# One kernel, one change: attention weights divided by each head's largest coefficient, the product with V in four column groups, and multiply-adds and tanh over two key blocks at a time

## What is computed

```python
q = (x @ Wq.T + bq).reshape(B, L, H, hd).transpose(0, 2, 1, 3)   # k, v likewise
sim = jnp.einsum('bhid,bhjd->bhij', q, k) / jnp.sqrt(hd) / (abs(temperature)[0] + 0.1)
scores = 0
for fi, freq in enumerate([31.0, 37.0, 41.0, 43.0, 47.0]):
    scores = scores + alpha[h, fi] * jnp.sin(TWO_PI * sim / freq + phi[h, fi])
w = jax.nn.sigmoid(scores)
w = w / (jnp.sum(w, axis=-1, keepdims=True) + 1e-10)
out = jnp.einsum('bhij,bhjd->bhid', w, v)                         # then Wo, bo, layer norm
```

## Time and profile before

| | us |
|---|---|
| median of 3 runs (7797.35 to 7801.88) | 7801.56 |
| the profiled execution | 7801.02 |
| its span in the trace | 7799.3 |
| projection and setup, to the first fill | 467.9 |
| attention, 467.9 to 6921.0 | 6453.1 |
| last stage | 878.3 |

### The profile page before, as it was taken

How to read it: one execution, slowest core, us unless ns; L and a number is a source line. 1 busy time by engine, 2 the same in 40 slices (tenths; PEclk the granted TensorE clock), 3 DMA queues, 4 the chain that set the end, 5 groups by cost and what they waited for, 6 DMA issues and landing times. The chain is left out here.

```text
span 7799.3 us, 138640 instructions
## 1 busy us (share of the span) xinstructions
PE 6920.1 (89%) x48057; PEld 4266.5 (55%) x48057; DVE 6862.6 (88%) x7370; ACT 5959.1 (76%) x6386; POOL 155.7 (2%) x217
## 2 busy tenths in 40 slices
PE   6459999999999999999999999999999999955555
PEld 3235555555555555555555555555555555534554
DVE  5659999999999999999999999999999999967775
ACT  1058888888888888888888888888888888841112
POOL 0000000000000000000000000000000000000000
PEclk8779999999999999999999999999999999976666
DMA  7921111111111111111111111111111111121110
GB/s 305 355 73 39 38 39 40 40 39 38 38 38 38 40 40 40 39 38 38 37 38 40 40 40 38 38 38 37 38 40 40 39 38 37 38 52 39 40 40 18
DMA packets 312136, 420.90 MB, mean 54 GB/s; under 512 B 156084, under 2 KB 185684, under 8 KB 311064
## 3 DMA queue, kind: packets, MB, share of 16 engines
q1 hardware_dynamic: 306712, 414.98, 16.8%
q0 software_dynamic: 5376, 5.30, 0.3%
HBM read 275.19 MB, written 144.83 MB: 54 GB/s over the span
## 5 line engine op out<-in xcount | busy, mean ns | idle before, releaser
L562 DVE SCALAR_TENSOR_TENSOR a_weight<-a_wave,a_head_c,a_weight 128x1024 f32<-128x1024 f32 x4096 | 5263.3, 1285 | 426.7 <-ACT a_wave L537 286.6
L537 ACT ACTIVATE a_wave<-a_ps_turn 128x1024 f32<-128x1024 f32 x5120 | 4926.0, 1033 | 733.2 <-PE a_ps_turn L465 733.2
L465 PE MATMUL a_ps_turn<-a_q_r,a_k_r 64*128 64x512 f32 x20480 | 3768.0, 413 | 308.6 <-ACT a_wave L537 204.9
L465 PE MATMUL a_ps_turn<-a_q_r,a_rounder 64*128 64x512 f32 x20480 | 3206.4, 391 | 0.0
L465 PEld LDWEIGHTS a_ps_turn<-a_q_r,a_k_r 64*128 64x128 f32 x20480 | 1922.3, 184 | 2170.2 <-ACT a_wave L537 1567.0
L465 PEld LDWEIGHTS a_ps_turn<-a_q_r,a_rounder 64*128 64x128 f32 x20480 | 1931.9, 185 | 271.2
L531 ACT ACTIVATE a_weight<-a_weight 128x1024 f32<-128x1024 f32 x1024 | 1097.0, 1071 | 2.4 <-DVE a_weight L562 2.4
L485 PE MATMUL a_ps_out<-a_weight,a_v_r 128*32 128x512 f32 x4096 | 1077.3, 605 | 3.9 <-ACT a_weight L531 2.4
L586 DVE TENSOR_SCALAR a_weight<-a_wave,a_head_c 128x1024 f32<-128x1024 f32 x1024 | 764.5, 747 | 55.9 <-ACT a_wave L537 55.9
L485 PEld LDWEIGHTS a_ps_out<-a_weight,a_v_r 128*32 128x32 f32 x4096 | 147.5, 107 | 376.1 <-ACT a_weight L531 328.8
L444 POOL COPY a_head_c<-a_table 128x5 f32 (+1 forms) x128 | 64.3, 503 | 6332.7 <-DVE a_weight L562 6332.7
(11 more groups left out here) (210 smaller groups left out, 1895.7 us busy)
## 6 DMA issues: line engine op xcount, KB each, us to landing
q_d<-p_q_hl SPq DMA_DIRECT2D x80, 1024.0 KB, 8.5
a_q_r<-q_d SPq DMA_DIRECT2D x256, 320.0 KB
a_k_r<-k_d SPq DMA_DIRECT2D x512, 128.0 KB
a_q_r<-q_d SPq DMA_DIRECT2D x256, 160.0 KB
k_d<-p_k_hl SPq DMA_DIRECT2D x8, 4096.0 KB, 15.5
a_k_r<-k_d SPq DMA_DIRECT2D x512, 64.0 KB
o_d<-a_out SPq DMA_DIRECT2D x256, 34.0 KB
p_x_in<-in_L_attn_x SPq DMA_DIRECT2D x8, 1024.0 KB, 17.4
```

What stands on the lines that cost most here:

```text
L465: last = nc.tensor.matmul(ps_turn[SLOT[f]][:, half, :], exact(w(rows[half])), exact(q_r[rows[half], k, f, :]), start=(i == 0), stop=(i == 3))
L537: nc.scalar.activation(wave[:, s % 2, f, :], ps_turn[SLOT[f]][:].rearrange("p a b -> p (a b)"), ACT.Sin, scale=TURN_IN).then_inc(sines, 1)
L562: return v.scalar_tensor_tensor(weight[:, s % RING, :], wave[:, s % 2, f, :], head_c[:, k, f:f + 1], weight[:, s % RING, :], ALU.mult, ALU ...
```

## The change

1. **Coefficients.** A chain of 45 small steps on DVE at the start of `project_qkv` makes a table `tab` of 16 heads: the frequency with the largest |alpha| changes places with frequency 0, and alpha, 1/freq and phi with it; the other four coefficients are divided by that largest one, and in place 0 stands half of it. The phases' reduction, until now seven steps in the attention's setup, is part of the chain. The scale of q comes from a tile `rate` with one column a frequency, which SP loads back through HBM, instead of constants.
2. **Multiply-adds.** The wave in place 0 has the coefficient 1, so its scaling goes: the first multiply-add takes wave 1 times its coefficient plus wave 0. `wave` and `weight` hold two units (a pair), and each of the four multiply-adds of a pair runs over 2048 columns. The wait is for the sine of the pair's second unit.
3. **tanh** runs over 2048 columns in place, with the scale read from `head_c` (half of the largest coefficient). It stands between sines 3 and 4 of the odd units.
4. **The product with V** is issued in the even units, for the pair two back: four matmuls, two units times two halves of the queries, each to its own 32 columns of the array. `ps_out` and `out` use 128 partitions; `o_d` holds two sums a head, which the last stage loads separately and adds: den in one small addition and num in one of 2048 columns.

The order of fills and sines is unchanged.

```diff
+                for i in range(3):
+                    step(v.tensor_tensor(work[0], tab[:, i, :], first, ALU.mult))
+                    step(v.tensor_tensor(work[1], tab[:, i, :], other, ALU.mult))
+                    step(v.tensor_copy(work[2][:, 0:1], tab[:, i, 0:1]))
+                    step(v.tensor_reduce(tab[:, i, 0:1], work[0], AX.X, ALU.add))
+                    step(v.scalar_tensor_tensor(tab[:, i, 1:NF], first[:, 1:NF], work[2][:, 0:1], work[1][:, 1:NF], ALU.mult, ALU.add))
...
-                        nc.vector.tensor_scalar(q_hl[:, f, 0, :].bitcast(F32R), whole, 1.0 / FREQS[f], None,
+                        nc.vector.tensor_scalar(q_hl[:, f, 0, :].bitcast(F32R), whole, rate[:, m, f:f + 1], None,
                                                 ALU.mult).then_inc(q_step, 1)
...
-                    for j in range(2):
-                        last = nc.tensor.matmul(ps_out[VP * j:VP * (j + 1), :], v_r[:, k, t, :],
-                                                weight[:, t % RING, halved(j)], start=(t == 0), stop=(t == U - 1))
+                    for c in range(4):
+                        last = nc.tensor.matmul(ps_out[VP * c:VP * (c + 1), :], v_r[:, k, t + c // 2, :],
+                                                weight[:, t // 2, c // 2, halved(c % 2)], start=(t == 0), stop=(t == U - 2))
                     last.then_inc(weighted, 1)
...
-                        if s >= 2 and main(g):
-                            times_v(n - 2, s - 2, g, k)
-                        if s < 2 and after(g):
-                            times_v(n - 2, U - 2 + s, g - 1, 1 - k)
+                        if s in (4, 6) and main(g):
+                            times_v(PAIRS * g + s // 2 - 2, s - 4, g, k)
+                        if s in (0, 2) and after(g):
+                            times_v(PAIRS * g + s // 2 - 2, U - 4 + s, g - 1, 1 - k)
...
-                            if f == 4 and (after(g) or s >= 1) and (main(g) or s == 0):
-                                act.wait_ge(summed, n)
-                                tile = weight[:, (s - 1) % RING, :]
-                                nc.scalar.activation(tile, tile, ACT.Tanh, scale=0.5).then_inc(squashed, 1)
+                            if f == 4 and s % 2 and (after(g) or s > 1) and (main(g) or s == 1):
+                                p = PAIRS * g + s // 2 - 1
+                                act.wait_ge(summed, p + 1)
+                                tile = weight[:, (s // 2 - 1) % PAIRS, :, :].rearrange("p a l -> p (a l)")
+                                nc.scalar.activation(tile, tile, ACT.Tanh, scale=head_c[:, k if s > 1 else 1 - k, 0:1]).then_inc(squashed, 1)
...
+                    for i in range(PAIRS):
+                        n, p = g * U + 2 * i + 1, g * PAIRS + i
+                        if i == 2 and after(g):
+                            dve.wait_ge(weighted, PAIRS * g)
                             wait_pos(dve, stored[1 - k], stores_before(g, k))
-                            v.tensor_copy(out[:, 1 - k, :], ps_out[0:2 * VP, :]).then_inc(out_ready, 1)
+                            v.tensor_copy(out[:, 1 - k, :], ps_out[:]).then_inc(out_ready, 1)
...
+                            wait_pos(dve, weighted, p - RING + 1)
+                            dve.wait_ge(sines, NF * n + 2)
+                            add_wave(i, k, 1, both(wave[:, i % 2, 0, :, :])).then_inc(added, 1)
+                            for f in range(2, NF):
                                 dve.wait_ge(sines, NF * n + f + 1)
-                                add_wave(n, s, k, f).then_inc(added, 1)
+                                dve.wait_ge(added, 3 * p + f - 1)
+                                add_wave(i, k, f, both(weight[:, i, :, :])).then_inc(summed if f == NF - 1 else added, 1)
...
+                        step_f(v.tensor_tensor(den[:, 2, :], den[:, 0, :], den[:, 1, :], ALU.add))
+                        step_f(v.tensor_scalar(den[:, 3, :], den[:, 2, :], float(L), 2 * EPS_DEN, ALU.add, ALU.add))
+                        v.reciprocal(den[:, 4, :], den[:, 3, :]).then_inc(S["den_ready"], 1)
+                        step_f(v.tensor_tensor(flat(num[:, 0, :, :]), flat(num[:, 0, :, :]), flat(num[:, 1, :, :]), ALU.add))
```

168 lines of the change are left out of this document (94 added, 74 removed).

## The result

The median of four runs of the changed kernel is 8204.31 us (8202.87 to 8205.89), against 7799.87 us for the kernel before (four runs, 7797.35 to 7801.88): a ratio of 1.0519, 95% interval 1.0501 to 1.0537. The forecast was 8195.

What follows compares the result with a forecast made beforehand. Bound taken: PE's loop through PSUM slot 1, 6.30 us a key block, not PE's total work. Attention +371, projection +4 and +7, last stage +10, together 392 more than 7801: 8193, rounded 8195 us; range 8085 to 8380 us.

Steps and rivals of the forecast that it cites:

- The PE loop and the ACT loop through slot 1: Attention, per key block: PE's fills, product and sine 1, 6.30 us; ACT's sines, tanh and fill 1, 6.01 us, hidden.
- The odd unit: Attention, a pair's key block with the wide tanh and no product: 6.94 us, PE idle 1.6 us before fill 1.
- The even unit: Attention, a pair's key block with the product and no tanh: stays at 6.30 us, product in four groups 0.98 us.
- The copy's wait: Attention, PE's first product of a head waits for DVE's copy of the last head's result: 0.36 us a head.
- DVE's 2.5 us a pair worth nothing: Attention: wider multiply-adds and dropped scalings save DVE about 2.5 us a pair, which gains nothing, as DVE wasn't the bound.
- The attention: Whole attention stage: 53.3 us a head, 2.9 more, over 128 heads +371 us.
- The projection: Projection stage: +4 us for the coefficient steps before PE's first turn of x, +7 us for pointer operands.
- The last stage: Stage after attention: extra loads and additions of den and num, +10 us, between 5 and 30.
- Rival (b): Attention: PE's work is the bound, not the loop, so a pair takes 11.62 us; 7320 us in all, chance 0.07.
- Rival (a): Product with V: four column groups don't run at once, product 1.84 us, +440 us, 8635 in all; chance 0.09.
- rival (c): Attention: no change, the pair stays at 12.60 us, tanh 0.64 us shorter than forecast; 7822 us in all, chance 0.02.
- Rival (d): Attention: PE's granted clock falls to 1.2 GHz as PE idles, +9.3 us a pair, some 12900 us; chance 0.01.

Runs made afterwards that it cites:

- e1: Changed kernel with the product with V moved from the even units to the odd ones, which have the tanh: 7555.7 us, ratio 0.9687 to the kernel before.
- e3: Changed kernel with the tanh moved from before sine 4 of the odd unit to behind it: 8017.9 us, ratio 1.0281 to the kernel before.
- e9: Changed kernel with fills in the order of the sines, PSUM slots 0, 1, 2 in turn, product behind an odd unit's fill: 7100.3 us.
- e6: Changed kernel with eight multiply-adds of 1024 columns a pair instead of four of 2048: 8199.9 us, ratio 1.0518 to the kernel before.
- e11: Changed kernel with PSUM slots in turn (e9), with eight multiply-adds of 1024 columns a pair instead of four of 2048: 7133.9 us.
- e10: Kernel before, with the PSUM slots in turn and the new fill order of e9, nothing of the change: 7532.7 us, ratio 0.9658.
- e7: Changed kernel with the product's four matmuls issued twice, in the even units: 8645.2 us, ratio 1.1086 to the kernel before.
- e8: Kernel with the product in the odd units (e1), with the product's four matmuls issued twice: 7704.2 us, ratio 0.9874 to the kernel before.

## Why the prediction was right, step by step

- **The PE loop and the ACT loop through slot 1** were read from the earlier trace rows. e1, e3 and e9 change only the order of things around slot 1 and move the time by -649, -186 and -1104 us. This is shown, not only argued.
- **The odd unit**, 6.94 us by the sum, took 6.95: the tanh lets the next sine start after 1.89 us (3069.99 to 3071.88; 1.88 forecast), and PE waits 1.56 (1.6 forecast).
- **The even unit** stayed at 6.30: the product in four groups spans 1.06 us as in two. From its start to the next fill it takes 1.00 us (3065.02 to 3066.02), 0.98 in the earlier trace rows. The estimate by the Trainium skill's figure for three column tiles ("TensorE: Matmul & The Clock Gate", section "Why this matters for your kernels") was at least 1.08 us and 8246 in all; the trace stays below it, so for these fp32 matmuls the measurement decides.
- **The copy's wait**: 0.36 us a head forecast, 0.31 measured (the even unit of 6.61 against 6.30).
- **DVE's 2.5 us a pair worth nothing**: e6 and e11 show it for the width. That they are worth nothing in the changed kernel holds only as long as slot 1 sets the pace; with the loop open the scalings count (e10).
- **The attention**: 371 us forecast, 381 measured. A head differs by 53.31 - 50.36 = 2.95 us where I had rounded to 2.9, which is 378 in all; the rest lies at the stage's two ends.
- **The projection**: +11 forecast, +5.5 measured. The tables landed at 3.1 us and not at 4, and a small step took 0.18 us, so that PE's first turn of x came at 13.64, +1.7 instead of +4. The pointers made the scalings and multiply-adds of q 58 ns longer each (691 to 749 and 1220 to 1278), 9.4 us in all, and DVE's waits for the stores of q fell from 118.0 to 112.2 us, so some 3.6 us of them are left where I had put 7.
- **The last stage**: +10 forecast, +15 measured, and the +10 was near by luck, as its terms were not these. I had 4 us for the loads, 2.5 for the two additions and 0.5 for each later batch. Nearly all of it lies in batch 0; the later batches keep their 99 us. There the loads land 7.0 us later (POOL's operation on x starts 46.2 us behind the last copy, and 39.2 before). The small addition takes 0.3 us, and the wide one lies beside PE's work and adds nothing. The other 7.2 us stand nowhere in my sum. 4.2 of them are one small DVE operation:

```profile
7353.69 0.29 DVE L1084 TENSOR_TENSOR den<-den 128x128 f32<-128x128 f32 x1 [12.59 <-DMA x_in<-in_L_attn_x]
7353.74 4.59 POOL L797 TENSOR_TENSOR x_in<-x_in,rows 128x2048 f32<-128x2048 f32 x1 [28.98 <-DMA x_in<-in_L_attn_x]
7354.02 4.40 DVE L1085 TENSOR_SCALAR den<-den 128x128 f32<-128x128 f32 x1
```

The addition of `den` that the change puts first pushes the next operation behind the start of POOL's long one, and it takes 4.40 us. In the kernel before it started 0.05 us ahead of POOL and took 0.23:

```profile
6959.92 0.23 DVE L1048 TENSOR_SCALAR den<-den 128x128 f32<-128x128 f32 x1 [9.39 <-DMA x_in<-in_L_attn_x]
6959.97 4.55 POOL L761 TENSOR_TENSOR x_in<-x_in,rows 128x2048 f32<-128x2048 f32 x1 [25.66 <-DMA x_in<-in_L_attn_x]
```

The Trainium skill has a rule on this ("SBUF — State Buffer", section "SBUF: two separate sides"): DVE and GpSimd share a pair of ports as an exclusive lock, and whichever starts first of a GpSimd operation and a DVE operation in a 2-port mode (or with two inputs in SBUF, against a GpSimd operation that reads SBUF) holds it for the whole instruction. The trace agrees here, with 4.2 us. It doesn't tell which mode the operation ran in, and in batch 1 the addition of `den` took 5.45 us though its row starts 0.79 us before POOL's (7434.09 and 7434.88), so the order of the rows' starts isn't all.

The other 3.0 us are PE's first product with Wo, in the changed kernel and before:

```profile
7364.88 6.72 PE L855 MATMUL A<-woa_t,o_t 128*128 128x256 f32 x16 [1.57 <-DVE o_t L1078]
```

```profile
6966.54 3.72 PE L819 MATMUL A<-woa_t,o_t 128*128 128x256 f32 x16 [1.50 <-DVE o_t L1042]
```

The granted clock was 0.55 over the first of them and 1.00 over the second. After the attention it had gone to the lower level (1.2 GHz) in both, and came back 63 us behind the last copy in the changed kernel and 45 us behind it in the one before.

Rival (b), that PE's work is the bound, is out by e1, which has the same work in 649 us less. Rival (a) is out by the product's row and e7, and rival (c), no change, by the odd unit's 6.95 us. Rival (d) is out for this kernel: the granted clock is 1.00 over its attention stage. It is in every other run that has a trace too, but in e8 it fell for eleven short stretches (last section). What the forecast didn't see is that the same change gains once its two long pieces lie in the same unit; its own sum had all that was needed for that.

## What to carry to other kernels

Where an engine pair hands buffers back and forth, write down for each buffer the loop that goes through it, with the order of both engines, and let the longest loop set the round. A long piece on one engine and a long piece on the other should lie in the same round of the loop, where one hides the other, and not in alternate rounds, where both are paid: that was 649 us here (e1). If relieving a busy engine brings nothing, look whether buffers used in turn open the loop: here that was worth 1104 us with the change and 267 without it.
